# A vision block on one core: an image's output in slices beside the scan of the next image, and GpSimd makes five of a pass's 24 drives in place of four

## The reference, cut to what matters

```python
xz = x_seq @ W_in
x, z = (xz[..., :D_INNER], xz[..., D_INNER:])          # D_INNER = 192
x = _silu(_causal_conv(x, conv_w, conv_b))
proj = x @ W_xproj
dt = jax.nn.softplus(proj[..., :DT_RANK] @ W_dt + b_dt)
Bm = proj[..., DT_RANK:DT_RANK + D_STATE]              # D_STATE = 16
Cm = proj[..., DT_RANK + D_STATE:]
# the scan, one step per token
dA = jnp.exp(dt_t[:, :, None] * A)
h = dA * h + dt_t[:, :, None] * B_t[:, None, :] * x_t[:, :, None]
y = jnp.einsum('bds,bs->bd', h, C_t)
...
return y * _silu(z) @ W_out
```

## Time and profile before

| | value |
|---|---|
| median of 3 runs | 6110.16 us |
| the profiled execution's own time | 6104.23 us |
| its span in the profile | 6102.4 us |
| up to the scan loop (convolution, pointwise, LayerNorm, first preparation) | to about 904 us |
| the 64 passes | about 904 to 5832 us |
| `output`, 64 slices | about 5832 to 6102 us |
| busy share of the span | DVE 88%, POOL 81%, PE 78%, ACT 53% |

### The profile page before, as it was taken

One profiled execution on the slowest core, in us unless ns is written; L12 is line 12 of the kernel. 1 busy time (PEld: TensorE's weight loads), 2 busy tenths in 40 slices (PEclk: granted clock), 3 DMA queues, 4 the chain that ended last, 5 costly groups with the idle time before them and its releaser, 6 DMA issues. The chain is left out here.

```text
span 6102.4 us, 74088 instructions
## 1 busy us (share of the span) xinstructions
PE 4730.4 (78%) x17356; PEld 1206.1 (20%) x17356; DVE 5353.6 (88%) x3584; ACT 3221.6 (53%) x5155; POOL 4946.7 (81%) x2339
## 2 busy tenths in 40 slices
PE   7999737777777777777777777777777777777788
PEld 6776211111111111111111111111111111111122
DVE  3224729999999999999999999999999999999953
ACT  1226635555555555555555555555555555555533
POOL 0000429999999999999999999999999999999965
PEclk9999877666666666666666666666666676666689
DMA  1002745555555555555555555555555555555599
GB/s 34 27 27 82 224 122 182 183 183 183 183 181 182 181 180 179 184 179 182 180 182 180 181 181 182 181 181 181 182 183 183 183 183 183 183 183 183 183 263 273
DMA packets 351021, 1048.26 MB, mean 172 GB/s; under 512 B 66820, under 2 KB 101430, under 8 KB 300556
## 3 DMA queue, kind: packets, MB, share of 16 engines
q1 hardware_dynamic: 334976, 1022.36, 52.8%
q10 hardware_dynamic: 16012, 25.53, 1.3%
HBM read 836.01 MB, written 211.63 MB: 172 GB/s over the span
## 5 line engine op out<-in xcount | busy, mean ns | idle before, releaser
L1267 POOL TENSOR_TENSOR hc<-hring,c_rep 128x1024 f32<-128x1024 f32 x1539 | 3602.2, 2356 | 245.8 <-DVE hring L1230 235.2
L1230 DVE TENSOR_TENSOR_SCAN hring<-decay,carry,u_ps 128x1024 f32<-128x1024 f32 x1283 | 2971.8, 2333 | 0.0
L1035 PE MATMUL u_ps<-stack_b,w_spread 48*128 48x512 bf16 x2568 | 1117.4, 527 | 953.0 <-DVE hring L1230 951.8
L1125 ACT ACTIVATE decay<-dt_rep,w_a 128x1024 f32<-128x1024 f32 x1285 | 1469.8, 1146 | 571.0 <-DVE hring L1230 570.1
L1212 DVE TENSOR_TENSOR u_ps<-u_ps,u_rep 128x1024 f32<-128x1024 f32 x1284 | 1551.4, 1208 | 92.6 <-PE u_ps L1035 89.3
L1053 PE MATMUL y_ps<-hc,w_gather 128*32 128x512 f32 x6144 | 1170.8, 846 | 55.3 <-POOL hc L1267 55.3
L1125 ACT ACTIVATE u_ps<-dt_rep,w_a 128x1024 f32<-128x1024 f32 x257 | 287.4, 1118 | 979.4 <-DVE hring L1230 979.4
L1077 PE MATMUL prep_ps<-xn,w_conv 128*128 128x512 f32 x792 | 618.8, 875 | 73.0 <-DMA xn<-xn_scr 71.4
L1035 PEld LDWEIGHTS u_ps<-stack_b,w_spread 48*128 48x128 bf16 x2568 | 155.6, 102 | 2536.9 <-DVE hring L1230 1823.3
L582 POOL TENSOR_TENSOR xs<-xc_ln,rs 96x512 f32<-96x512 f32 x64 | 90.3, 1411 | 682.5 <-ACT rs L566 668.2
L1254 POOL TENSOR_TENSOR drive_p<-u_rep,b_rep 128x1024 f32<-128x1024 f32 x258 | 609.1, 2361 | 27.7 <-DMA u_rep<-u_scr 27.7
(11 more groups left out here) (108 smaller groups left out, 3926.8 us busy)
## 6 DMA issues: line engine op xcount, KB each, us to landing
dt_rep<-dt_scr SPq DMA_DIRECT2D x194, 1024.0 KB, 5.9
u_rep<-u_scr SPq DMA_DIRECT2D x194, 1024.0 KB, 7.9
c_rep<-bc_scr SPq DMA_DIRECT2D x260, 512.0 KB, 5.4
b_rep<-bc_scr SPq DMA_DIRECT2D x130, 512.0 KB, 4.4
xn<-xn_scr SPq DMA_DIRECT2D x132, 384.0 KB, 6.5
y_scr<-y_sb SPq DMA_DIRECT2D x768, 64.0 KB, 4.3
xn<-xn_scr SPq DMA_DIRECT2D x132, 256.0 KB, 6.7
dt_scr<-dt_sb SPq DMA_DIRECT2D x260, 128.0 KB, 2.1
```

Source lines behind the costliest of these rows:

```text
L1035: mm = nc.tensor.matmul(u_ps[nv % NSLOT][:, sl], w["spread"][:, q, :], upper(stack_b[drv][:, sl]), start=True, stop=True)
L1125: nc.scalar.activation(to[:, :], dt_rep[r][:, b, :], ACT.Exp, scale=w["a"][:, col:col + 1]).then_inc(decay_ready, 1)
L1230: nc.vector.tensor_tensor_scan(hring[nv % NHR][:, ::step], factor[:, ::step], term[:, ::step], carry[:, drv, nv:nv + 1], ALU.mult, ALU.add ...
L1267: nc.gpsimd.tensor_tensor(hc[nv % NHC][:, :], hring[nv % NHR][:, :], c_rep[q][:, :], ALU.mult).then_inc(c_applied, 1)
```

## The change

Three things.

1. The output of images 0 to 6 moves into the scan loop: from pass 8 on (`OUT_LAG` = 8), each pass handles one 512-token slice of the image before, 56 slices in all. SP loads it at m=14 of the pass ahead (7 DMAs); PE makes z at m=21 and 22 into `prep_ps`, and ACT copies it out; ACT takes its silu at m=0, in place, under the table that is loaded for `xa`; DVE adds the two directions at m=1 (`y_fwd`) and gates at m=3 (`y_bwd`), both 128x768 with both operands in SBUF; PE projects at m=7 into `prep_ps`, ACT copies at m=8, SP stores at m=10. Channels are laid out as 128 + 64 rows, the last 64 in two halves of the tokens, so that a slice is 128x768. Only the last image goes through `output`, in 8 slices.
2. `POOL_UNITS` becomes (2, 6, 11, 15, 19): POOL makes five drives of a pass, DVE 19. Its drives then stand at m=18, 22, 3, 7, 11 (before: 18, 22, 2, 15).
3. The input convolution moves one position later, because the bank `prep_ps` is now used at m=7 and 8 by the projection. Its first step also waits for `res_ready`.

```diff
-POOL_UNITS = (2, 6, 10, 23)
+POOL_UNITS = (2, 6, 11, 15, 19)
...
-        CONV_AT = ((8, 9, 10), (12, 13, 14), (16, 17, 18))
+        CONV_AT = ((9, 10, 11), (13, 14, 15), (17, 18, 19))
...
-        B_AT = tuple(11 + i for i in range(len(POOL_QUADS)))
+        B_AT = (13, 12)
...
+        SLICE_AT, Z_AT = 14, (21, 22)
+        SUM_Y_AT, GATE_AT, PROJECT_AT, RES_AT, OUT_STORE_AT = 1, 3, 7, 8, 10
+        SLICE_DMAS = 7
...
-            with eng.Fori(0, ITERS) as it:
+            def iteration(it, gates, slices):
...
+            with eng.Fori(0, CHUNKS - 1) as it:
+                iteration(it, (False, False), (False, False))
+            iteration(CHUNKS - 1, (False, True), (False, False))
+            with eng.Fori(CHUNKS, ITERS) as it:
+                iteration(it, (True, True), (True, True))
...
+                        sp.dma_start(xz[:, :], d["xn_scr"][image, :, bass.ds(at + HALO, SL)]).then_inc(slice_in, 16)
+                        for to, scr in ((y_fwd, d["y_scr"][0]), (y_bwd, d["y_scr"][1])):
+                            sp.dma_start(to[:, 0:SL], scr[image, 0:P, bass.ds(at, SL)]).then_inc(slice_in, 16)
+                            for s in range(2):
+                                sp.dma_start(to[64 * s:64 * s + 64, SL:], scr[image, P:DI, bass.ds(at + s * (SL // 2), SL // 2)]).then_inc(slice_in, 16)
...
+                            if g == 0 and slicing:
+                                pe.wait_ge(res_ready, pn - 1 - OUT_LAG)
...
+                def slice_out(m, k, it, dr):
+                    if m == PROJECT_AT:
+                        pe.wait_ge(gated, k + 1)
+
+                        pe.wait_ge(prep_out, NPREP * (k + OUT_LAG + 2))
+                        for s in range(2):
+                            cols = slice(s * (SL // 2), (s + 1) * (SL // 2))
+                            nc.tensor.matmul(prep_ps[0:C, cols], w["out"][:, 0, :], y_bwd[:, cols], start=True, stop=False)
+                            mm = nc.tensor.matmul(prep_ps[0:C, cols], w["out"][:, 1 + s, :], y_bwd[:, SL:], start=False, stop=True)
+                        mm.then_inc(projected, 1)
...
+                        if slicing:
+                            act.wait_ge(z_out, 2 * (pn - OUT_LAG))
+                            nc.scalar.activation(z_sb[:, :], z_sb[:, :], ACT.Silu).then_inc(z_silu, 1)
...
+                def slice_out(m, k, it, dr):
+                    if m == SUM_Y_AT:
+                        dve.wait_ge(slice_in, 16 * SLICE_DMAS * (k + 1))
+                        nc.vector.tensor_tensor(y_fwd[:, :], y_fwd[:, :], y_bwd[:, :], ALU.add).then_inc(y_sum, 1)
+                    if m == GATE_AT:
+                        dve.wait_ge(y_sum, k + 1)
+                        dve.wait_ge(z_silu, k + 1)
+                        nc.vector.tensor_tensor(y_bwd[:, :], y_fwd[:, :], z_sb[:, :], ALU.mult).then_inc(gated, 1)
```

More of the change, by code:

```diff
@@ L88, in over_slices, with over_last @@
     image(B - 1, last=True)
+def over_last(eng, *stages):
+    most = max(lead for lead, _ in stages)
+    for s in range(-most, NS):
+        for lead, what in stages:
+            if 0 <= s + lead < NS:
+                what(s + lead)
 def after(eng, sem, count):
@@ L858, in run @@
                             elif kind == "prep":
-                                what(m, p + 1, it + dr, 1 - dr)
-                            else:
-                                what(m, p + 2, it + 1, dr)
+                                what(m, p + 1, it + dr, 1 - dr, slices[dr])
+                            elif kind == "conv":
+                                what(m, p + 2, it + 1, dr, slices[dr])
+                            elif kind == "gate" and gates[dr]:
+                                what(m, p + 1 - OUT_LAG, it + dr, 1 - dr)
+                            elif kind == "slice" and slices[dr]:
+                                what(m, p - OUT_LAG, it, dr)
                     for kind, what in tasks:
@@ L1188, in back, with gate, slice_out @@
                     nc.scalar.copy(y_sb[:, :], y_ps[:, :]).then_inc(y_ready, 1)
+                def gate(m, k, it, dr):
+                    if m == Z_AT[0]:
+                        wait(act, gated, k, k)
+                        act.wait_ge(z_made, 2 * k + 1)
+                        nc.scalar.copy(z_sb[:, 0:SL], prep_ps[:, :]).then_inc(z_out, 1)
+                    if m == Z_AT[1]:
+                        act.wait_ge(z_made, 2 * k + 2)
+                        nc.scalar.copy(z_sb[:, SL:], prep_ps[:, 0:SL // 2]).then_inc(z_out, 1)
+                def slice_out(m, k, it, dr):
+                    if m == RES_AT:
+                        act.wait_ge(projected, k + 1)
+                        wait(act, out_stored, 16 * k, k)
+                        nc.scalar.copy(res[:, :], prep_ps[0:C, :]).then_inc(res_ready, 1)
                 act.wait_ge(zeroed, 1)
                 load_exp_ln(nc)
-                run(act, ("back", back), ("front", front), ("prep", prep), ("conv", conv))
+                run(act, ("back", back), ("front", front), ("prep", prep), ("slice", slice_out), ("conv", conv), ("gate", gate))
             @block.vector
```

157 lines of the change are left out of this document (105 added, 52 removed).

## The result

| | before | after |
|---|---|---|
| median, us (4 runs each) | 6108.77 (6106.02 to 6110.85) | 6181.02 (6179.20 to 6185.19) |
| span of the profiled execution, us | 6102.4 | 6179.2 |
| first drive to end of last scan, us | 4928.1 | 5226.8 |
| end of last scan to end of span, us | 270.6 | 46.0 |
| a pass without a slice, us | 76.8 | 78.9 and 78.1 in turn |

The ratio is 1.0119, with an interval of 1.0107 to 1.0131: the change makes the kernel slower by 1.2%. The forecast was 6080. The output stage lost what was said; a pass with a slice grew by 5.1 us where 3.6 was said. The time of a kernel is the median of its fast runs; one of the ten runs of the kernel with the narrow projection was slow (7004.3 us) and is left out.

What follows compares the result with a forecast made beforehand. The passes were taken to cost DVE's line, the output the DMAs. Terms +202 (56 x 3.6), -9, +1.5 and -224 gave -30 us: 6074 for the profiled execution, a median of 6080; range 5975 to 6180.

Steps and rivals of the forecast that it cites:

- The output stage: Behind the last scan: only the last image's 8 slices remain, 46.7 us in place of 270.6, -224.
- DVE's line: In the passes: scans at 2.25 us and drives at 1.12 add up to 4903 of 4928 us.
- The sum and the gate: DVE's two slice instructions at m=1 and m=3, with waits for POOL's port: 2.2 us a pass.
- Rival B: At m=1 POOL keeps the port, the sum waits 4.7 us more; +4.4 a pass, 6326 us; chance 0.12.
- The projection at unit 13: PE's projection at m=7 delays unit 13's spread, so DVE's drive waits: 2.5 us a pass.
- C: PE at low clock at every projection, 3.3 in place of 2.5: 6125, up to 6150 us; chance 0.17.
- A: Projection at m=7 mostly hidden, clock high, -1.3 a pass: 6007 us, 5940 with no wait; chance 0.22.
- I cost this at 0: POOL's fifth drive and its lag of some 5 us at m=3 to 13, covered by four states: 0.
- up to 1 or 2 us a pass: Bound on the cost of POOL's lag behind DVE if the cover of the four-state ring is gone.
- -9: Eight passes without a slice: DVE loses one drive of 1.12 us in each, -9 us.
- The convolution, one position later, has the gap of unit 15: 0: On PE in the passes: the moved convolution fits where no spread for POOL's unit is due; cost 0.
- The sum again: A pass with a slice: 54.0 + 19 x 1.12 + 0.4 + 2.2 + 2.5 = 80.4 against 76.8, +3.6.

Runs made afterwards that it cites:

- narrow projection: The four projection matmuls of a slice 8 columns wide in place of 256: against the changed kernel 6120.37 us; in the 5975.06 us kernel 6052.44 us.
- the kernel with the convolution off the odd positions: Changed kernel, odd POOL units kept, convolution at (9, 10, 12), (13, 14, 16), (17, 18, 20), three of nine steps at odd positions: 6108.91 us.
- the kernel with the units alone: Kernel before with POOL units 2, 6, 11, 15, 19, no slices, convolution where it was: 6104.92 us, ratio 0.9998.
- either remedy: Changed kernel with POOL units 2, 6, 10, 14, 18 (5980.30 us), or with three convolution steps at odd positions in place of six (6108.91 us).
- the best kernel: Changed kernel with POOL units 2, 6, 10, 14, 18 and convolution at (9, 10, 12), (13, 14, 16), (17, 18, 20): 5975.06 us, 0.9782.

## Why the prediction was wrong, by its steps

- **The output stage was right.** 46.7 us forecast, 46.0 measured; -224 of 270.
- **DVE's line was right.** 1540 scans and the drives at the same prices; a late pass adds up from the earlier trace rows and the waits.
- **The sum and the gate were right,** 2.2 forecast and 1.97 measured, and the point in time as well: the sum finds 0.24 us of POOL's multiply left, where 0.25 was forecast. Rival B did not happen in the changed kernel, but its mechanism is real, and its price of 4.7 us is what the two sums of the kernel with the convolution off the odd positions show (5.88 - 1.11 = 4.8).
- **The projection at unit 13: the number was right by luck,** 2.5 forecast and 2.62 measured. The forecast is a mean over both clocks, 0.62 x 3.3 + 0.38 x 1.2, on the ground that the two levels would drift over the passes. They did not: in 54 of the 56 passes the projection takes the same 3.66 us, which is the low level, and the drive waits 2.6. So C's condition came true. Its price of 3.3 was 0.7 too high: the gather ended at 1.7 and not at 2.0, the four matmuls took 3.67 and not 3.8, and the spread behind them ran at the high clock, 0.6 and not 1.03; nor did unit 12's late drive give 0.2 back. The two errors cancel. A did not hold. The narrow projection shows that 1.9 of the wait is the width, and the kernels with unit 10 in place of 11 that some 1.35 goes with the odd unit; the two overlap.
- **"I cost this at 0", POOL's lag and fifth drive, failed.** The bound that stood beside it, "up to 1 or 2 us a pass", was the right one for the passes without a slice: the kernel with the units alone has passes of 76.8, not 75.7. The step that failed looked only at who waits for POOL directly. No wait of DVE ends there; PE's gather waits for POOL, and the spread stands behind the gather. Price: 8 x 1.1 = 9 us, the whole of the "-9". Most of that, too, goes with the odd units: with five even ones and the convolution where it was, the first eight passes are 76.1.
- **"The convolution, one position later, has the gap of unit 15: 0" failed.** This is the large one. It asked whether the convolution had a gap, and not what else PE does in it. With a unit of POOL at 15 and 19, the spreads of 17 and 21 have 5.6 us, and the move put six of nine convolution steps, not three, beside a gather. Measured at units 17 and 21: 1.56 + 0.43 = 1.99 a pass, and 1.7 in a pass without a slice; taken away alone by either remedy, so it needs both the move and the odd units.
- **The sum again:** a late pass lacked 1.99, and had 0.4 of small waits and 0.2 for the port too much, and 0.1 too little at unit 13: 80.4 + 1.5 = 81.9. 56 x 1.5 = 84, and 8 x 2.8 = 22 for the first passes. With 106 the 6074 of the forecast become 6180, which is the profiled execution's 6180.95. The 6 us from there to the forecast of 6080 were not needed: this execution lies at the median of its runs.
- C's words "with more small waits at units 12, 17 and 21" named two of the three places, but without the cause: the same convolution step stood at another position before, and with it back at an even one the waits at 17 and 21 are gone. The low clock of the rows beside them (1.93, 1.94 and 1.90) may have a part in their size. The mean clock of the passes rose, 0.71 where the earlier trace rows had 0.69.
- The range ended at 6180, 1 us short. It took in the price of the clock and not the two edits that were put at 0, which were never given their upper bound.

**What is open.** Why POOL keeps the port for two more instructions in one case and lets DVE in after one in another. In the ten kernels with the sum at position 1, 479 of the 560 sums are short (1.1 us, a few 1.2) and 81 long (5.8 to 6.3). At the short ones POOL's next instruction starts 0.23 to 0.34 us behind the sum's start, at the long ones 0.31 to 0.78; in the kernel with the sum at position 2 it would have been 1.5, and it was served after one. The lag of POOL at the moment may decide, or which of its instructions are already issued; no run here held the one fixed and moved the other. Open as well is why the projection stays at the low clock in nearly every pass.

## What to carry to other kernels

When one engine hands a unit of work to another, go to the consumers of the units behind it: the producer that feeds them has now less time, and what an unrelated edit puts into that gap can come out as a wait. An edit that only moves work by one position gets a row of the sum of its own, checked against every wait of the engine that executes it, and if its cost can't be shown to be hidden its upper bound goes into the range. And where two engines share a port, a faster pass can cost more than it gives: try neighbouring phases before keeping one. And a mean of two clock levels is a doubtful price for one place: here the projection came back at the same level in 54 of 56 passes.

## What the hardware showed that I had not expected

- A DVE instruction of 768 elements with both operands in SBUF took 1.1 or 5.9 us beside a busy POOL, and hardly anything between, at the same place of the program: long in 19 of 56 with the convolution off the odd positions, in 18 and 21 of 56 in the best kernel with the later and with the narrow projection, in none of the changed kernel. The Trainium skill (SBUF — State Buffer, "Who interferes with whom") has the exclusive lock, and that issue order decides who blocks. The lock agrees. The order does not by itself: the sum of 2750.31 had been waiting for 0.4 us when POOL's fifth multiply started, and still came after it and the next.
- Twice a kernel with less to wait for was the slower one: 6052 with the narrow projection against 5975 with the full one, and 6033 with the projection at position 8, the same work and a shorter wait.
- Moving three units of GpSimd by one position each, with the same work on every engine, was worth 3.2% (6181.02 against 5980.30).
